# Attention and FFN kernel: q's product ahead of the transpositions, output products of two groups in one run

## The reference

```
xn   = layernorm(x) * g_norm
q    = l2norm(xn @ Wq per head) * q_scale ;  k = l2norm(k) * k_scale,  [k, v] = xn @ Wkv, with one null key and value ahead
p    = softmax(8 q k^T + relative bias, causal)
y    = layernorm(concat_heads(p v) @ Wout) * g_out
out  = x + down(quantise(silu(gate(xq)) * up(xq)))     with xq = quantise(y), one scale over all of y
```

## Time and profile before

| | |
|---|---|
| median of 3 runs | 299.69 us (299.69 to 299.98) |
| the profiled execution | 299.08 us, its span 297.3 us |
| PE busy | 257.9 us (87%) |
| DVE busy | 238.1 us (80%) |
| ACT busy | 230.0 us (77%) |
| POOL busy | 204.6 us (69%) |
| granted TensorE clock, mean | 0.970 |

### The profile page before, as it was taken

One profiled execution on the slowest core, in us unless ns is written; L12 is line 12 of the kernel. 1 busy time (PEld: TensorE's weight loads), 2 busy tenths in 40 slices (PEclk: granted clock), 3 DMA queues, 4 the chain that ended last, 5 costly groups with the idle time before them and its releaser, 6 DMA issues.

```text
span 297.3 us, 7308 instructions
## 1 busy us (share of the span) xinstructions
PE 257.9 (87%) x2161; PEld 203.5 (68%) x2162; DVE 238.1 (80%) x969; ACT 230.0 (77%) x781; POOL 204.6 (69%) x394
## 2 busy tenths in 40 slices
PE   0769999999999999999999999999999989975270
PEld 0427777787888778877887888788878767751060
DVE  2768978798879878888888798787877788869893
ACT  1554978888898899889988988889888897259380
POOL 2277979788878887887888888788877785013300
PEclk9989999999999999999999999999999999999857
DMA  4179100000000000000000000000000020000013
GB/s 142 33 191 264 21 1 2 1 2 1 3 0 2 4 1 2 0 3 1 2 0 4 3 0 2 0 4 0 2 0 4 1 73 3 2 0 0 1 37 110
DMA packets 13084, 6.89 MB, mean 23 GB/s; under 512 B 1954, under 2 KB 12914, under 8 KB 13043
## 3 DMA queue, kind: packets, MB, share of 16 engines
q1 hardware_dynamic: 11874, 6.03, 7.7%
q10 hardware_dynamic: 1168, 0.36, 0.6%
HBM read 5.31 MB, written 1.07 MB: 21 GB/s over the span
## 4 chain that ended last, share of the span: by engine, by line
PE 60%; DVE 20%; POOL 8%; issue 5%; DMA 4%; ACT 2%; SPq 1%; POOLq 0%; DVEq 0%; ACTq 0%
PE bank L904 14%; PE front L881 7%; PE bank L855 7%; PE back L947 7%; PE bank L744 6%; POOL prob L448 6%; PE back L881 5%; PE front L947 4%; DVE score L1276 4%; DMA g1b<-in_L_cond_g_dram 4%; PE bank L760 3%; DVE oT L1266 2%; DVE hmax L1428 2%; DVE oT L1464 2%; DVE yn L1299 1%
## 5 line engine op out<-in xcount | busy, mean ns | idle before, releaser
L589 ACT ACTIVATE prob<-score,negmax 128x258 f32<-128x258 f32 (+1 forms) x256 | 113.4, 449 | 17.8 <-DVE negmax L1276 17.7
L448 POOL TENSOR_SCALAR prob<-prob,rrow 128x258 f32<-128x258 f32 x254 | 107.9, 443 | 22.0 <-DVE rrow L1284 20.1
L401 POOL TENSOR_TENSOR rq<-qn,neghalf 128x8 f32<-128x8 f32 x32 | 53.3, 1666 | 2.7
L589 ACT ACTIVATION_READ_ACCUMULATOR prob<-score,negmax 128x1 f32 x256 | 49.2, 192 | 0.0
L904 PE MATMUL bank<-pT,val 128*64 128x256 f32 x496 | 47.1, 332 | 0.0
L1276 DVE CUSTOM_DVE_ANT_0 score<-front,bias 128x258 f32<-128x258 f32 (+1 forms) x128 | 38.2, 354 | 8.0 <-PE front L881 7.8
L904 PEld LDWEIGHTS bank<-pT,val 128*64 128x64 f32 x496 | 30.8, 136 | 19.3 <-ACT pT L599 9.9
L1145 DVE TENSOR_REDUCE qn<-sq 128x8 f32<-128x512 f32 x32 | 21.9, 684 | 23.7 <-ACT sq L535 23.7
L1276 DVE CUSTOM_DVE_ANT_0 score<-back,bias 128x258 f32<-128x258 f32 (+1 forms) x128 | 38.0, 353 | 0.1
L855 PE MATMUL bank<-wout,oT 128*128 128x128 f32 x256 | 36.7, 287 | 1.2 <-DVE yn L1299 1.1
L599 ACT COPY pT<-back 128x384 f32<-128x384 f32 x62 | 28.8, 481 | 9.0 <-PE back L947 8.6
(11 more groups left out here) (203 smaller groups left out, 465.0 us busy)
## 6 DMA issues: line engine op xcount, KB each, us to landing
bias<-relative_table SPq DMA_DIRECT2D x8, 256.0 KB, 5.0
out_dram<-prob SPq DMA_DIRECT2D x4, 256.0 KB, 3.0
X<-in_x_dram SPq DMA_DIRECT2D x1, 896.0 KB, 13.9
prob<-in_L_cond_Wq_dram SPq DMA_DIRECT2D x1, 512.0 KB, 5.4
wout<-in_L_cond_Wout_dram SPq DMA_DIRECT2D x1, 512.0 KB, 15.1
prob<-in_L_ffn_w_down_dram SPq DMA_DIRECT2D x1, 176.0 KB, 2.4
X<-in_x_dram SPq DMA_DIRECT2D x1, 128.0 KB, 4.3
prob<-in_L_ffn_w_gate_dram SPq DMA_DIRECT2D x1, 128.0 KB, 2.2
```

Source lines behind the costliest of these rows:

```text
L401: pool.tensor_tensor(dst, src, neghalf[:, 0:width], ALU.pow).then_inc(done, 1)
L448: pool.tensor_scalar(prob[:, par, h, cols], prob[:, par, h, cols], rrow[:, par, h, t:t + 1], 1.0, ALU.mult, ALU.mult).then_inc(normed, 1)
L589: act.activation(prob[:, par, h, cols], score[:, h % 4, cols], ACT.Exp, scale=-1.0, bias=negmax[:, par, h, t:t + 1], accum_out=rowsum[:, p ...
```

## The change

Nothing is computed otherwise, and no instruction of an engine's arithmetic is added or removed. The order changes:

- TensorE: q_make stands ahead of turn 0 and not behind turn 3. y_products are issued only in groups whose `summed` is odd (g = 1 and g = 3), for two groups at once. `values` waits for the transposed heads 0 and 1 ahead of its first 8 products and for heads 2 and 3 ahead of the other 8, and no longer for all four at its start.
- ScalarE: q_square stands behind the exponentials of heads 0 and 1 and ahead of pT_evac, for the quarter made in this very group; it stood at the start of the next group.
- VectorE: q_norm2 follows in the same group, ahead of qT_evac. q_normalise moves from between the two score pairs to the group's start; there it is ahead of oT_copy (in g = 2 behind it), and in g = 2 y_normalise stands ahead of oT_copy. y_stats moves ahead of q_norm2.
- GpSimd: normalise of heads 2 and 3 of the group before comes first, then x_power, y_power (now in g = 1), q_power, k_power (a group earlier), and normalise of heads 0 and 1.

```diff
 # GpSimd, group(s)
-                if s.kT is not None:
-                    k_power(s.kT)
-                if s.g == 2 and s.prev is not None:
-                    y_power(s.prev)
-                if s.g == 3 and s.b + 3 < B:
-                    x_power(s.b + 3)
-                if s.quarter is not None and s.quarter >= 4:
-                    q_power(s.quarter, s.quarter % 4)
                 if s.turned is not None:
                     normalise(heads(s.turned)[2:4])
                 if s.at == 2:
                     x_power(2)
+                if s.g == 3 and s.b + 3 < B:
+                    x_power(s.b + 3)
+                if s.g == 1 and s.prev is not None:
+                    y_power(s.prev)
+                if s.made is not None:
+                    q_power(s.made, s.made % 4)
+                if s.kv is not None:
+                    k_power(s.kv)
                 normalise(heads(s.at)[0:2])
 # GpSimd, ending()
-                y_power(B - 2)
 # ScalarE, group(s)
-                if s.quarter is not None and s.quarter >= 4:
-                    q_square(s.quarter, q_ps)
 ...
                 exponent(heads(s.at)[1])
+                if s.made is not None:
+                    q_square(s.made, q_ps)
                 if s.turned is not None:
                     pT_evac(s.turned, 0)
 # TensorE, values(at)
-                if at == LOOP:
-                    pe.wait_ge(pTe_ready, GH)
-                else:
-                    pe.wait_ge(pT_ready, GH * (at if at > LOOP else at + 1))
 ...
                 for pair in range(2):
+                    if at == LOOP:
+                        pe.wait_ge(pTe_ready, 2 * pair + 2)
+                    else:
+                        pe.wait_ge(pT_ready, GH * (at - 1 if at > LOOP else at) + 2 * pair + 2)
 # TensorE, group(s)
-                if s.summed is not None:
-                    y_products(s.summed, 0)
-                    y_products(s.summed, 1)
+                if s.summed is not None and s.summed % 2:
+                    for at in (s.summed - 1, s.summed):
+                        y_products(at, 0)
+                        y_products(at, 1)
                 if s.g == 1 and s.prev is not None:
                     y_null(s.prev)
+                if s.made is not None:
+                    if s.made % 4 == 0:
+                        if s.first:
+                            pe.wait_ge(wq_low, 1)
+                        pe.wait_ge(xT_low, s.next)
+                    q_make(s.made, s.made % 4, s.made // 4 % 2, q_ps)
                 if s.turned is not None:
                     turn(s, 0)
                     turn(s, 1)
 ...
                     turn(s, 3)
-                if s.made is not None:
-                    if s.made % 4 == 0:
-                        if s.first:
-                            pe.wait_ge(wq_low, 1)
-                        pe.wait_ge(xT_low, s.next)
-                    q_make(s.made, s.made % 4, s.made // 4 % 2, q_ps)
 # VectorE, group(s)
-                if s.quarter >= 4:
-                    q_norm2(s.quarter, s.quarter % 4)
-                if s.summed is not None:
-                    oT_copy(s.summed)
                 if s.g == 2 and s.prev is not None:
                     y_normalise(s.prev)
+                    oT_copy(s.summed)
+                if s.quarter >= 4:
+                    q_normalise(s.quarter, s.quarter % 4, q_ps)
+                if s.summed is not None and not (s.g == 2 and s.prev is not None):
+                    oT_copy(s.summed)
+                if s.at == 1:
+                    xT_split_low(1, 1)
                 if s.first:
                     dve.wait_ge(ld_bias[s.g], 16 * 2)
                 score_pair(heads(s.at)[0:2])
 ...
                 if s.kT is not None:
                     k_normalise(s.kT)
-                if s.quarter >= 4:
-                    q_normalise(s.quarter, s.quarter % 4, q_ps)
                 score_pair(heads(s.at)[2:4])
 ...
                 invert(heads(s.at)[0:2])
+                if s.g == 1 and s.prev is not None:
+                    y_stats(s.prev)
+                if s.made is not None:
+                    q_norm2(s.made, s.made % 4)
                 if s.quarter > 2:
                     qT_evac(s.quarter, s.quarter % 4, s.quarter // 4 % 2)
                 if s.at == 1:
-                    xT_split_low(1, 1)
                     x_stats(2)
 ...
-                if s.g == 1 and s.prev is not None:
-                    y_stats(s.prev)
 # VectorE, ending()
+                y_normalise(B - 2)
                 oT_copy(LOOP - 2)
-                y_normalise(B - 2)
```

## The result

The changed kernel takes 303.36 us (median of 4 runs, 302.43 to 303.99) after 299.69: a ratio of 1.0131, 95% interval 1.0096 to 1.0165. It is slower, 3.7 us by the medians, which on their own give a ratio of 1.012.

The account below looks back on a forecast made before the run. TensorE was taken as the bound, with some 1.2 us a batch of waiting. First groups -1.7, groups 4 to 8 +0.7, five batches +3.8, group 28 -0.2, group 29 +0.7: +3.3, forecast 302.9 us, range 298.9 to 304.8.

Parts of the forecast that it names:

- Groups of two sizes: Groups g = 0 and 2 lose y_products but can't shrink to TensorE's content; a batch takes 29.52 us after 28.71.
- floor of a short group: Way from scores through VectorE, GpSimd or ScalarE to the next scores: 6.51 us in g = 2, 6.74 in g = 0.
- The term for rq in g = 0: Late q_make in g = 3 brings rq 0.23 us after g = 0's start, making that group 6.88 us.
- The order of q_normalise and oT_copy: Both ahead of VectorE's first score operation, which starts 1.32 us after the group's start, 0.21 later than before.
- The long groups: g = 1 and g = 3: TensorE's content plus 0.15 us of waiting for the last pT copy, 8.32 and 7.81 us.
- a head paid once: One run of 16 y_products might save 0.1 us in each of 11 long groups; the forecast counted nothing.
- The split wait: Before each group's values TensorE waits 0.08 us for the last pT copy; splitting the wait removes that.
- The first groups: Up to group 4 the new GpSimd order saves 1.7 us; at group 8 the new kernel is 1.0 ahead.
- Rival A: Short groups run at TensorE's content, a batch 28.0 us, about 294.5 in all; chance 0.17.
- Rival B: A draw: short groups of 6.3 to 6.4 us, a batch level, 298.5 to 300 in all; chance 0.08.
- Rival C: Late q_power delays turn 0 or VectorE's scores by 0.3 us in 11 short groups: 306 us; chance 0.09.

Follow-up runs that it names:

- e2: The kernel before with y_products of two groups in one run of every second group, nothing else changed: 307.51 us, ratio 1.0313.
- e3: The changed kernel with oT_copy ahead of q_normalise on VectorE in every group: 299.65 us, ratio 1.0045 to the kernel before.
- e1: The changed kernel with y_products issued in every group again, all else as changed: 300.79 us, ratio 1.0081 to the kernel before.
- e5: The kernel before with only the wait of values split in two, as in the change: 298.0 us, ratio 1.0007.
- e7: The changed kernel with y_products in every group, oT_copy ahead of q_normalise and the old single wait of values: 307.8 us, ratio 1.0327 to the kernel before.

## Why the prediction was right, and where not

The forecast was 302.9 and the measurement is 303.36. The direction and the mechanism (a short group can't shrink to TensorE's content) were right. That the number is within 0.5 is in part luck: the forecast added 3.3 us, all in the loop, and the loop grew by 4.7. The two profiled executions differ by 4.5, with 0.6 more in the prologue and 0.8 less behind the start of group 30, where the time from VectorE's last instruction to the end was 3.4 after 4.7; the medians differ by 3.7. In later runs the kernel before had medians of 298.28 and 297.99, 1.4 and 1.7 below the one compared with here. By the steps of the forecast:

*Groups of two sizes.* Right, as mechanism (e2) and in the floor of a short group: 6.51 and 6.74 predicted, 6.51 and 6.76 in e3. In the changed kernel's g = 2 it is 6.71, since rq is late there too. For that group I had no term. Its rq is made in g = 1, where y_power now stands ahead of q_power:

```profile
156.86 0.71 POOL L401 TENSOR_TENSOR ors<-omv,neghalf 128x2 f32<-128x2 f32 x1
157.67 0.24 POOL L399 TENSOR_SCALAR qn<-qn 128x8 f32<-128x8 f32 x1
157.99 1.66 POOL L401 TENSOR_TENSOR rq<-qn,neghalf 128x8 f32<-128x8 f32 x1
```

q_norm2 was done at 156.96 (VectorE's timeline) and q_power began at 157.67, behind y_power. rq was there at S + 0.88, and q_normalise could have started at S + 0.73.

*The term for rq in g = 0.* Mis-sized. I put rq at S + 0.23, from 4.54 us between q_make and the end of q_power in the earlier trace rows; it came at S + 0.50, and g = 0 took 7.18 and not 6.88. The 4.54 held for a GpSimd that was free: without x_power it is 4.5 in the changed kernel too, and g = 0 is 6.83 (group 24). I gave x_power no term, though the change puts it ahead of q_power. It stood in the way because late scores held it back: in e3, with the scores 0.45 earlier, it is done in time and g = 0 is 6.76 with or without it. The order of q_normalise and oT_copy, which I named as a cost of 0.21, was worth 0.42 in g = 0 and 0.20 in g = 2 (e3).

*The long groups.* 8.32 and 7.81 predicted, 8.09 and 7.66 measured. In g = 1 a run of 16 y_products takes 1.89 up to y_null (152.19 to 154.08), not 2.00. The Trainium skill (TensorE: Matmul & The Clock Gate, Part 2, Step-by-step) has weight loads pulled ahead of running matmuls; by that rule I gave 0.1 for a head paid once and then went by the rows. The trace agrees with it and with the 0.1 here. In g = 3 the run takes 1.80 (167.00 to 168.80), but there q_make follows it, and ahead of q_make 8 products take 0.91 (144.56 to 145.47 in e1), so twice that is no more than 1.82. The waiting for the last copy of pT was also smaller than 0.15: values start to scores are 1.49 in g = 1 (157.28 to 158.77 in the timeline) after 1.45. For g = 3 the two together would give 7.5, so some 0.15 of its 7.66 is content that I had put too low; no run isolates it.

The errors, +0.3 in g = 0, +0.2 in g = 2 and -0.4 in the long groups, nearly cancel: 29.64 a batch, 29.52 predicted.

*The split wait.* Costed as a gain of 0.08 a group on today's waits: there is none (e5). Its worth is to replace q_make's cover (e7).

*The first groups.* Measured from group 0's scores, group 4 starts 1.3 earlier (26.46 after 27.76), where I had 1.7; at group 8 it is 0.1 ahead (56.70 after 56.82) where I had 1.0: the batch from group 4 to 8 grew by 1.2 (30.25 after 29.06) and not by 0.7. At group 30 the change is 4.7 behind, where I had 3.3.

*Rival A* (short groups at TensorE's content) is refuted by e2: 1.0 us of products left two groups and their length did not move. It would have held only for a kernel in which nothing but TensorE bounds a group. *Rival B* fell on its condition, short groups of 6.3 to 6.4: they were 6.7 and 7.2. *Rival C* is in part what happened: q_power ending in the next group did make VectorE's scores slip by 0.4 in g = 0, though TensorE waited for nothing at turn 0.

## What to carry to other kernels

A share of 87% on one engine says nothing about what happens when its work is lumped: work out, for the lightest stage, the way through all engines from one use of a buffer to the next, and compare that with the engine's content. A step that is reordered on one engine (x_power, y_power here) needs a term of its own for what now stands behind it. When a producer is moved earlier so that its consumer falls into the same round, look for the ring that this closes, and put what doesn't belong to the ring ahead of the wait (oT_copy here: one swap of two lines, worth 3.4 us of the loop). Edits can be worth more together than one by one: 1.8 us of the loop (e1), 3.4 (e3) and 9.1 both, since each left a wait that the other removes.

## What the runs showed of the hardware

- The time of a run of fp32 products of 128 columns with their weight loads hangs on what follows: 8 take 1.00 us up to y_null or a transposition and 0.91 up to q_make's 512-column products, 16 take 1.89 and 1.80. With the same product behind, one run of 16 saves 0.11 or 0.02 against two of 8.
- k_normalise, two vector instructions with both tensors in SBUF, takes 0.58 to 0.62 us, 0.75 (most groups g = 1 of e3) or 0.94 to 1.02, by the phase of GpSimd's multiplications beside it, without any wait shown. In the kernel before they begin 0.3 after it does, and it takes 0.59. The Trainium skill (GPSIMD Engine Reference, 1. Specifications) says that GpSimd shares its SBUF interfaces with VectorE and contends with its instructions of two SBUF inputs; these rows agree.
- The prologue, the same in all these kernels, ended between 25.2 and 27.5 us in nine profiles: a difference of 2 us between single profiles says nothing about a loop.
